# Where TensorE's projection pieces stand in a delta rule recurrence: behind small inverse products, or in longer runs

## The reference

```
q = l2norm(conv_silu(h @ Wq)) * DK**-0.5      # causal convolution over 4 tokens, then silu
k = l2norm(conv_silu(h @ Wk))
v = conv_silu(h @ Wv)
beta = sigmoid(h @ Wb) * 2 ;  g = -exp(A_log) * softplus(h @ Wa + dt_bias)
def step(S, (q_t, k_t, v_t, g_t, b_t)):
    S = S * exp(g_t)
    delta = (v_t - k_t @ S) * b_t
    S = S + outer(k_t, delta)
    return S, q_t @ S
x = x + (rmsnorm(o) * norm_weight * silu(h @ Wg)) @ Wo
```

## Time and profile before

| what | value |
|---|---|
| median of 3 runs | 2404.33 us (2402.9 to 2404.34) |
| span of the profiled execution | 2401.2 us |
| TensorE busy | 2317.9 us (97%), 19896 matmuls |
| VectorE busy | 2111.3 us (88%) |
| ScalarE busy | 1425.7 us (59%) |
| GpSimd busy | 1066.8 us (44%) |
| recurrence, steps 0 to 60 | 84 to 2020 us |

### The profile page before, as it was taken

The page is one execution under the profiler, slowest core; times in us unless marked ns, Lnnn a source line. Parts: engine busy times, 40 slices in busy tenths (PEclk is TensorE's granted clock), DMA queues, the critical chain, the costliest instruction groups (busy, mean ns, idle before and its releaser), DMA issues. The chain is left out here.

```text
span 2401.2 us, 55407 instructions
## 1 busy us (share of the span) xinstructions
PE 2317.9 (97%) x19896; PEld 1640.4 (68%) x19896; DVE 2111.3 (88%) x4579; ACT 1425.7 (59%) x3891; POOL 1066.8 (44%) x1543
## 2 busy tenths in 40 slices
PE   5899999999999999999999999999999999888998
PEld 3677767777777777776767777777777776773554
DVE  8999999998989999999999999999999989648776
ACT  5566666656565666666666666665555555333665
POOL 3634354444434354545343544444343535214564
PEclk8999999999999999999999999999999999788999
DMA  5211122222212112222221222221111011002000
GB/s 139 64 45 47 39 53 52 55 53 55 53 50 48 47 45 63 61 64 62 57 61 41 60 58 64 62 64 38 38 33 34 19 36 22 17 19 119 23 23 27
DMA packets 289390, 120.76 MB, mean 50 GB/s; under 512 B 211510, under 2 KB 267094, under 8 KB 288604
## 3 DMA queue, kind: packets, MB, share of 16 engines
q1 hardware_dynamic: 289116, 117.21, 18.5%
HBM read 85.42 MB, written 31.74 MB: 49 GB/s over the span
## 5 line engine op out<-in xcount | busy, mean ns | idle before, releaser
L1450 DVE SCALAR_TENSOR_TENSOR d_y<-bank,d_cw,d_y 128x508 f32<-128x508 f32 (+2 forms) x576 | 421.9, 733 | 6.3 <-ACT d_y L1205 0.8
L794 POOL TENSOR_SCALAR d_ms<-d_sso 128x4 f32<-128x4 f32 x64 | 14.5, 226 | 573.6 <-ACT d_junk L1343 573.6
L778 POOL TENSOR_TENSOR d_V<-d_tok,d_kinv 128x640 f32<-128x640 f32 (+1 forms) x128 | 130.3, 1038 | 303.8 <-issue 301.9
L1628 DVE SCALAR_TENSOR_TENSOR x<-bank,x 128x512 f32<-128x512 f32 x256 | 172.3, 677 | 51.3 <-PE bank L1018 51.3
L1205 ACT ACTIVATE d_y<-bank,d_cw 128x512 f32<-128x512 f32 x192 | 131.2, 684 | 88.6 <-PE bank L859 86.1
L1328 ACT ACTIVATE d_thg<-bank 128x384 f32<-128x384 f32 x128 | 62.2, 486 | 199.3 <-PE bank L973 196.9
L1614 DVE SCALAR_TENSOR_TENSOR d_on<-d_O,d_rn,d_gate 128x192 f32<-128x192 f32 x256 | 154.8, 663 | 0.0
L824 POOL TENSOR_SCALAR d_K<-d_tok,d_Em 128x96 f32<-128x96 f32 x256 | 151.3, 607 | 0.0
L1254 ACT ACTIVATE d_tok<-bank 128x384 f32<-128x384 f32 x256 | 125.5, 490 | 36.1 <-PE bank L875 32.1
L1212 ACT ACTIVATE d_th<-d_y 128x512 f32<-128x512 f32 x192 | 121.6, 634 | 41.3 <-DVE d_y L1456 34.8
L1471 DVE SCALAR_TENSOR_TENSOR d_yv<-d_th,d_y 128x512 f32<-128x512 f32 x128 | 98.2, 767 | 52.1 <-ACT d_th L1212 44.5
(11 more groups left out here) (341 smaller groups left out, 7115.4 us busy)
## 6 DMA issues: line engine op xcount, KB each, us to landing
lt_blocks<-d_LT SPq DMA_DIRECT2D x64, 256.0 KB, 2.4
d_fw<-turned_gate_w SPq DMA_DIRECT2D x32, 256.0 KB, 3.0
d_XT<-x_blocks SPq DMA_DIRECT2D x128, 64.0 KB, 2.3
d_X<-x_blocks SPq DMA_DIRECT2D x128, 64.0 KB, 2.3
d_fw<-turned_val_w SPq DMA_DIRECT2D x32, 256.0 KB, 3.0
d_fw<-turned_out_w SPq DMA_DIRECT2D x32, 256.0 KB, 2.8
d_st<-in_L_attn_Wg_dram SPq DMA_DIRECT2D x16, 384.0 KB, 4.2
ternary<-d_ft SPq DMA_DIRECT2D x48, 128.0 KB, 2.1
```

Of the source, the lines that this page charges most:

```text
L778: last = nc.gpsimd.tensor_tensor(V[q][:, :, lo:hi], tok[q][:, :, at:at + hi - lo], over(kinv[:, :], 2, hi - lo), ALU.mult)
L1450: nc.vector.scalar_tensor_tensor(out=yy[:, :, tap:], in0=pp[:, :, 0:P - tap], scalar=cw[:, ds(st.kp, 1), t, 3 - tap], in1=yy[:, :, tap:], ...
L1628: nc.vector.scalar_tensor_tensor(out=xs, in0=bank[(4, 7, 6, 5)[i]][:, :], scalar=1.0 / (SO * SW), in1=xs, op0=ALU.mult, op1=ALU.add).then_ ...
```

## The change

In steps with c > 0 the order of TensorE's instructions is changed; steps with c = 0 keep theirs. The first piece of the second projection stands ahead of `queries` instead of behind. Its second piece stands behind `x_16`, two follow `y_32`, one follows `x_32` and one the token turn after it. Two pieces of the third projection stand behind `y_join` and behind `x_join`, and four are left where six were.

```diff
                 else:
                     y_16(st)
+                    proj(1, 0, 6)
                     queries(st)
-                    proj(1, 0, 6)
                 x_16(st)
+                if c:
+                    proj(1, 1, 6)
                 pair_of(st, "ks_done", 0, 4, lambda i: key[:, i, :], lambda i: S[:, i, :], product=c > 0)
...
                     y_32(st)
-                    proj(1, 1, 6)
                     proj(1, 2, 6)
+                    proj(1, 3, 6)
                     x_32(st)
+                    proj(1, 4, 6)
                     turn(1)
-                    for part in (3, 4, 5):
-                        proj(1, part, 6)
+                    proj(1, 5, 6)
...
                 y_join(st)
+                if c:
+                    proj(2, 0, 6)
...
                 x_join(st)
+                if c:
+                    proj(2, 1, 6)
...
-                for part in range(4 if c == 0 else 0, 6):
+                for part in range(4 if c == 0 else 2, 6):
                     proj(2, part, 6)
```

## The result

The changed kernel takes **2389.85 us** (median of 5, 2389.58 to 2390.05), the kernel before 2404.33. The ratio is 0.9951 with a 95% interval of 0.9935 to 0.9966. That is 0.34 to 0.65% faster. I had forecast 2400.9 us, with a low end of 2399.3, and "within 0.2%". In a second comparison the changed kernel took 2388.61 us beside 2403.89, a ratio of 0.9934 (0.9918 to 0.9950). The prediction was wrong: the direction held, and so did the part at x_16, but the gain of 14.5 us was over four times the 3.4 us forecast, and most of it came from places where I had forecast none.

A forecast was written before the change was run, and what follows sets the result against it. TensorE's instructions, one after the other, were taken to bound the kernel: -0.10 + 0.01 = -0.09 us in 46 steps gives -4.1, less 0.7 lost, -3.4, so 2404.33 became 2400.9 us; 8-in-10 range 2399.3 to 2406.3.

The forecast's parts named there:

- y_16 to x_16: Stretch between these two small products on TensorE: 2.10 us before, 2.01 after, a gain of 0.09 to 0.10 a step.
- The boundary to the state products: From the piece behind x_16 to L985: taken as 0.00 over the piece's 0.43 us, as at the queries.
- The token turn, 0.01 over: Projection piece moved between x_32 and the token turn: its boundary to the turn costs 0.01 us over streaming.
- From a small product to a projection 0.59 against 0.58: Start to start, a small product followed by a projection takes 0.59 us, by a float32 product 0.58; adds 0.01.
- What comes late: Results needed behind the moved pieces: silu up to 0.77 us later, about a third expected to arrive, nothing lost.
- the tight place: TensorE's second pair of L985 with V, waiting for VectorE's last residual addition; 0.36 us lost if the whole 0.77 arrives.
- rival 2's narrow form: Late silu holds up L985 with V in 15 projecting c = 2 steps, 0.36 us each: +5.4, 2406.3 us; 8 in 100.
- The late Y16 in c = 1 steps: In seven second steps of a head x_16 waits for VectorE's Y16; 0.10 us each, 0.7 us together, is lost.
- Rival 1: Loads exposed behind pieces at three L985 boundaries, 0.10 us each in 46 steps: +13.8, time 2414.7 us; 5 in 100.
- Rival 4: More gain: all rounding to the good side and Y16 not late, -5.9, so 2398.4 us; 12 in 100.

## Why the prediction was wrong, point by point

- **y_16 to x_16, 2.10 to 2.01 us, gain 0.09 to 0.10.** Right: 2.02 us in the changed kernel, and 0.09 a step with this edit alone.
- **The boundary to the state products, "so I take 0.00 from there", bounded below by zero "since the streaming of the piece remains".** This step failed. The boundary itself was nearly right: piece to L985 0.44 us, 0.01 over. But I kept 1.40 and 0.76 us as what the state products cost wherever they stand, while 0.10 of each was the load exposed by the small product ahead. Three groups at 0.10 in each step were left out. The excluded end, a gain beyond zero, was where the result lay.
- **The token turn, 0.01 over.** The turn itself fell from 0.38 to 0.33 us by the same cause; I had read only the 0.44 ahead of it. One piece alone ahead of the turn saves 0.045 a step.
- **"From a small product to a projection 0.59 against 0.58", and so nothing to gain.** The numbers are right and the reading was wrong. Start to start across the boundary says nothing of a load that starts with its matmul. The price is in the next group. The page of before had it: the queries take 1.00 us between y_16 and a piece, and 0.99 between a piece and y_16, where the second pays at its end what the first pays at its front.
- **What comes late, "and that nothing is lost".** This failed too, in c = 2 steps. The silu was to come 0.77 later and came at 1172.16 - 1155.85 = 16.31 us into the step against 15.84, 0.47 later, since the groups ahead had become faster. TensorE wanted the V products 0.40 earlier and not 0.09. I had the tight place at the second pair; it was the first pair, which waits for the third addition. Before, this addition ended 0.48 us ahead of the pair. Now it ends 0.18 us later in the step (22.11 instead of 21.93 us), about a quarter of the 0.77 where I had expected a third, and the pair is wanted 0.40 earlier. So rival 2's narrow form came true in 14 c = 2 steps, at 14 x 0.40 = 5.6 us. That its price of 0.36 us is also the measured wait is luck: I had 0.31 for a late addition and 0.05 until the start, and it was 0.11 and 0.25, at another pair.
- **The late Y16 in c = 1 steps.** Right that the first stretch gains nothing there: x_16 starts 2.37 and 2.38 us into the step. These steps gain 0.31 and not 0.40.
- **Rival 1**, three exposed loads behind the pieces, is refuted by 0.44 us from piece to L985. Rival 4, more gain, pointed the right way but for another reason, rounding and an early Y16. The Trainium skill, page TensorE: Matmul & The Clock Gate, under what overlaps and what doesn't, says that loads overlap running matmuls only where the row group differs. Here a load of 96 rows runs 0.22 us beside a 128-row projection matmul, so the trace speaks against the rule in that form.

The sum as it is: -0.09 - 3 x 0.09 - 0.045 = -0.40 us; 15 steps with c = 3, 16 with c = 1 of which some less, one with c = 2, make -12.4 us. Of each step's 0.40 the prediction had 0.09; the three state groups and the turn, 0.31, are what it put at nothing.

## What to carry to other kernels

The cost of a boundary between two kinds of matmul must be read on both sides: how long the group ahead lasts until the next start, and how much longer the group behind lasts than the same group elsewhere. If the same products take 0.76 us in one place and 0.65 in another, the neighbours are the price, and a long matmul with nothing else to do belongs between them. When TensorE gets faster, look for the step in which another engine does extra work; a gain can be whole in one kind of step and missing in another.

## What the runs showed that I had not expected

- The time of the same kernel scatters with the mean granted clock of the execution. The kernel before, on one chip: 2388.74 us at 0.987, 2391.75 at 0.984, 2405.18 at 0.980, 29 executions in all. In the traces the low level (1.2 GHz, granted 0.5) stands in the first 120 us and behind step 61, where TensorE waits most, and in different stretches each time. A difference under 10 us between single executions says little, while the steps in between repeat within 0.01 us.
- The first pair with V started 0.25 to 0.29 us after the addition it waits for had ended, the second pair of a first-of-head step 0.05 to 0.06. A further wait stands behind the first one in the program ahead of the first pair. Whether that is the cause was not tried.
- Why a small product's load, and a wide load behind small products, doesn't run ahead was not tried either. The runs show only where it does and where it doesn't. Nor do they show why a token turn behind small products pays 0.05 us and a state group 0.10.
